# The loads of kept rows and of up's rows in the down stage: issued by SP instead of ScalarE

## The reference, cut to what matters

```
x = x + cross_attention(layernorm(x), ctx, mask)     # 16 batches of 64 tokens, 1601 keys
z = layernorm(x)                                     # 1024 tokens of 1024
s = silu(z @ w_gate.T)                               # 1024 x 2752
s = s with the 1376 smallest |s| of each row set to 0
x = x + (s * (z @ w_up.T)) @ w_down.T                # the down stage computes this product
x = x + mixture(layernorm(x))                        # top 2 of 8 low-rank experts
```

## Time and profile before

| | us |
|---|---|
| median of 3 runs (1389.53 to 1391.22) | 1389.76 |
| the profiled execution: its time | 1390.6 |
| the profiled execution: its span | 1388.8 |
| TensorE busy, of the span | 1338.2 (96%) |
| VectorE busy | 1019.0 (73%) |
| GpSimd busy | 894.5 (64%) |
| ScalarE busy | 804.5 (58%) |

### The profile page before, as it was taken

One profiled execution on the slowest core, in us unless ns is written; L12 is line 12 of the kernel. 1 busy time (PEld: TensorE's weight loads), 2 busy tenths in 40 slices (PEclk: granted clock), 3 DMA queues, 4 the chain that ended last, 5 costly groups with the idle time before them and its releaser, 6 DMA issues.

```text
span 1388.8 us, 30205 instructions
## 1 busy us (share of the span) xinstructions
PE 1338.2 (96%) x12535; PEld 990.2 (71%) x12535; DVE 1019.0 (73%) x1332; ACT 804.5 (58%) x1018; POOL 894.5 (64%) x561
## 2 busy tenths in 40 slices
PE   4999999999999999999999999999999999999897
PEld 3555555555555555589999998788888777887764
DVE  6888888888888888880000699996899885456555
ACT  6788888888888888843223742514234333343532
POOL 0799888888888888824433443242232798888571
PEclk9899999999999999999999999999999999999999
DMA  9022423232323232014336435797688799866452
GB/s 357 18 98 98 142 99 114 99 113 98 116 99 114 98 109 80 2 73 146 126 133 263 171 114 206 173 262 197 177 213 240 247 285 272 280 232 204 151 184 96
DMA packets 195586, 218.66 MB, mean 157 GB/s; under 512 B 96288, under 2 KB 169136, under 8 KB 191472
## 3 DMA queue, kind: packets, MB, share of 16 engines
q1 hardware_dynamic: 176736, 193.68, 43.4%
q10 hardware_dynamic: 18704, 22.96, 5.2%
HBM read 174.67 MB, written 41.94 MB: 156 GB/s over the span
## 4 chain that ended last, share of the span: by engine, by line
PE 77%; DVE 15%; ACT 3%; issue 2%; DMA 1%; POOL 1%; ACTq 0%; SPq 0%; POOLq 0%; DVEq 0%
PE fast_psum L2031 17%; PE fast_psum L2049 15%; PE fast_psum L2169 15%; PE fast_psum L2118 13%; PE fast_psum L2140 6%; PE fast_psum L2068 6%; DVE fast_below L1442 4%; PE fast_psum L2075 1%; DVE fast_near L1518 1%; DVE fast_top L1485 1%; PE fast_psum L2198 1%; PE fast_psum L2054 1%; PE fast_psum L2217 1%; DVE fast_near L1479 1%; DVE fast_near L1512 1%
## 5 line engine op out<-in xcount | busy, mean ns | idle before, releaser
L1372 DVE TENSOR_TENSOR fast_masked<-fast_psum,fast_mask_t 128x1024 f32<-128x1024 f32 (+1 forms) x416 | 488.4, 1219 | 72.4 <-PE fast_psum L2031 70.5
L1227 POOL TENSOR_TENSOR fast_pair<-fast_probs 128x1024 f32<-128x1024 f32 x192 | 456.9, 2383 | 96.9 <-PE fast_psum L2068 47.9
L1775 ACT ACTIVATE fast_probs<-fast_masked 128x1024 f32<-128x1024 f32 (+1 forms) x416 | 437.9, 1058 | 68.9 <-DVE fast_masked L1372 53.7
L1283 POOL TENSOR_TENSOR fast_d_lo<-fast_d_raw,fast_d_hi 128x256 fp32r<-128x256 f32 x252 | 217.7, 895 | 60.3 <-ACT fast_d_hi L1914 60.2
L2031 PE MATMUL fast_psum<-fast_qT,fast_kraw 32*128 32x256 f32 (+1 forms) x3328 | 247.1, 403 | 6.7 <-ACT fast_qT L1722 3.2
L2049 PE MATMUL fast_psum<-fast_probs,fast_vraw 128*32 128x256 f32 (+1 forms) x3328 | 226.6, 386 | 0.8 <-ACT fast_probs L1775 0.8
L2031 PEld LDWEIGHTS fast_psum<-fast_qT,fast_kraw 32*128 32x128 f32 (+1 forms) x3328 | 153.7, 182 | 93.2 <-DVE fast_masked L1372 53.9
L1260 POOL TENSOR_TENSOR fast_g_lo<-fast_g_raw,fast_g_hi 128x1408 fp32r<-128x1408 f32 x28 | 89.9, 3232 | 140.5 <-ACT fast_g_hi L1836 118.4
L2118 PE MATMUL fast_psum<-fast_g_hi,fast_z_hi 128*128 128x352 f32 x512 | 166.2, 325 | 0.0
L2118 PE MATMUL fast_psum<-fast_g_hi,fast_z_lo 128*128 128x352 f32 x512 | 165.9, 324 | 0.0
L1914 ACT CAST fast_d_hi<-fast_d_raw 128x1024 fp32r<-128x1024 f32 x66 | 69.3, 1051 | 165.8 <-PE fast_psum L2169 154.5
(11 more groups left out here) (174 smaller groups left out, 1930.5 us busy)
## 6 DMA issues: line engine op xcount, KB each, us to landing
fast_d_raw<-w_down SPq DMA_DIRECT2D x63, 512.0 KB, 4.3
fast_kraw<-ctx_t SPq DMA_DIRECT2D x32, 800.5 KB, 5.9
fast_vraw<-ctx_nat SPq DMA_DIRECT2D x16, 1536.0 KB
fast_g_raw<-w_gate_up SPq DMA_DIRECT2D x15, 1408.0 KB, 7.2
fast_mag<-s SPq DMA_DIRECT2D x9, 1376.0 KB, 8.3
fast_u_raw<-w_up_t SPq DMA_DIRECT2D x21, 512.0 KB, 6.5
u_t<-fast_u_out SPq DMA_DIRECT2D x42, 256.0 KB, 4.5
s<-fast_res SPq DMA_DIRECT2D x14, 704.0 KB, 3.8
```

Of the source, the lines that this page charges most:

```text
L1227: pool.tensor_tensor(pair[:, n % PAIR_BUFS], both[:, :, 0, :], both[:, :, 1, :], ALU.add).then_inc(paired, 1)
L1283: last = pool.tensor_tensor(low[rs, qs], d_raw[j][rs, qs], d_hi[j][rs, qs].bitcast(F32), ALU.subtract)
L1372: dve.tensor_tensor(into, of, m, ALU.add).then_inc(mask_added, 1)
L1775: act.activation(probs[0:r, g % RING, hp * HALF:(hp + 1) * HALF], masked[0:r, h % SLOTS, :], ACT.Exp).then_inc(exp_done, 1)
```

## The change

`load_factors` is moved out of ScalarE's program and takes the engine as its first argument. The first four loads are still issued by ScalarE. All others are issued by SP, at the same step n of its loop (for n+4), directly behind the weight load for n+3 and ahead of pieces, `load_x` and the loads of the last stage. The waits within are the same. Nothing else is changed.

```diff
--- before.py
+++ after.py
@@ -1012,6 +1012,27 @@
 
             return (0, 1) if t == 7 else (4, 5)
 
+        def load_factors(eng, n):
+            gi, k = divmod(n, IC)
+            if n >= TURNS:
+                eng.wait_ge(h_ready, n - TURNS + 1)
+            if k == 0:
+                stored = max(GROUPS[gi][-1] + 1, TILES - 2)
+                for j in range(2):
+                    eng.wait_ge(st_stored[j], 16 * QUARTERS * ((stored + 1 - j) // 2))
+            m, t0 = len(GROUPS[gi]), GROUPS[gi][0]
+            eng.dma_start(t_s[n % TURNS][0:rows(k), 0:m * P], s_t[k * P:k * P + rows(k), t0 * P:(t0 + m) * P]
+                          ).then_inc(ts_full[n % TURNS], 16)
+            if twice(n):
+                eng.dma_start(t_s[n % TURNS][UREST:P, 0:m * P], s_t[UF * P:I, t0 * P:(t0 + m) * P]
+                              ).then_inc(ts_full[n % TURNS], 16)
+                return
+            if gi == 0:
+                for i in (2 * k, 2 * k + 1):
+                    eng.wait_ge(u_stored[i % OUTS], 16 * (i // OUTS + 1))
+            eng.dma_start(t_u[n % TURNS][:, 0:m * P], u_t[k * P:(k + 1) * P, t0 * P:(t0 + m) * P]
+                          ).then_inc(tu_full[n % TURNS], 16)
+
         def load_k(sp, b):
             for u in range(2):
                 sp.dma_start(kraw[b % BUFS][:, u, :], ctx_t[2 * b + u]).then_inc(k_full[b % BUFS], 16)
@@ -1185,6 +1206,8 @@
             for n in range(STEPS):
                 if n + DS < STEPS:
                     load_down(n + DS)
+                if n + TURNS < STEPS:
+                    load_factors(sp, n + TURNS)
                 if n in DOWN_PIECE_AT:
                     store_piece(*DOWN_PIECE_AT[n])
                 if n in LOAD_X_AT:
@@ -1877,27 +1900,6 @@
                     for r in rounds:
                         compare(p, r)
 
-            def load_factors(n):
-                gi, k = divmod(n, IC)
-                if n >= TURNS:
-                    act.wait_ge(h_ready, n - TURNS + 1)
-                if k == 0:
-                    stored = max(GROUPS[gi][-1] + 1, TILES - 2)
-                    for j in range(2):
-                        act.wait_ge(st_stored[j], 16 * QUARTERS * ((stored + 1 - j) // 2))
-                m, t0 = len(GROUPS[gi]), GROUPS[gi][0]
-                act.dma_start(t_s[n % TURNS][0:rows(k), 0:m * P], s_t[k * P:k * P + rows(k), t0 * P:(t0 + m) * P]
-                              ).then_inc(ts_full[n % TURNS], 16)
-                if twice(n):
-                    act.dma_start(t_s[n % TURNS][UREST:P, 0:m * P], s_t[UF * P:I, t0 * P:(t0 + m) * P]
-                                  ).then_inc(ts_full[n % TURNS], 16)
-                    return
-                if gi == 0:
-                    for i in (2 * k, 2 * k + 1):
-                        act.wait_ge(u_stored[i % OUTS], 16 * (i // OUTS + 1))
-                act.dma_start(t_u[n % TURNS][:, 0:m * P], u_t[k * P:(k + 1) * P, t0 * P:(t0 + m) * P]
-                              ).then_inc(tu_full[n % TURNS], 16)
-
             def take_high(n):
                 gi, k = divmod(n, IC)
                 w = len(GROUPS[gi]) * P
@@ -1926,7 +1928,7 @@
                         compare(p, r)
                 if i == 2 * UF - 5:
                     for n in range(TURNS):
-                        load_factors(n)
+                        load_factors(act, n)
                 if i == 2 * UF - 3:
                     round_down(0)
                 if i == 2 * UF - 2:
@@ -1957,8 +1959,6 @@
             for n in range(STEPS):
                 if n >= 2:
                     take_high(n)
-                if n + TURNS < STEPS:
-                    load_factors(n + TURNS)
                 if n in ZT_AT:
                     take_zt(ZT_AT[n])
                 if n in PICK_AT:
```

## The result

The changed kernel takes 1395.22 us (median of 8 runs, 1391.57 to 1399.24), the kernel before beside it 1391.37 (8 runs, 1389.53 to 1393.79). The ratio is 1.0029 with a 95% interval of 1.0015 to 1.0043: about 4 us slower. Forecast were a median of 1390.3, half a us above the 1389.76 of the kernel before, and a range of 1387.0 to 1394.0. Of the 4.9 us between that median and 1395.22, 1.6 are the kernel before itself, which took 1391.37 here; 3.3 are what the forecast missed.

A forecast was written before the change was run, and what follows sets the result against it. TensorE was taken to bound the down stage, with 11.2 us of gaps. Terms 0 + 0 + 0 + 0.3 + 0.2 = +0.5 us took the profiled 1390.6 to 1391.1, median 1390.3, range 1387.0 to 1394.0.

The forecast's parts named there:

- What bounds the kernel: Down stage: TensorE is nearly always busy, so the change can pay only in its gaps, 11.2 us in all.
- ScalarE's side, 0: Some 49 us of issuing leave ScalarE, nearly all beside its other work, so nothing is gained: 0.
- the 5.95 us of the earlier trace: Sum of fourteen factor issues by ScalarE in the chain of waits, the most the change could gain there.
- rival B: Faster: ScalarE's issues are on the path, up to 5.95 us go, 1383.8, or 3.2 us, 1386.6; chance 0.14.
- The start, 0: Stage start: step 2's weights arrive when ScalarE's issues end, so removing the issues gives nothing: 0.
- Factors late, 0: SP issues factor loads later, but those of steps 6 and 14 still land before VectorE multiplies: 0.
- The steps with pieces, +0.3: Weights share SP's queue with factors; one pair delays them 1.4 us, under the cover: +0.3 us, bounds 0 and +3.6.
- a cover of 2.0: Time in hand in steps with pieces: 0.9 us from weight landing to `d_hi`, 1.1 more before TensorE starts.
- The 3.05 us of the earlier trace: Length of a weight issue on SP in the steps with pieces before the change, a queue without room.
- Step 25, +0.2: SP issues four last-stage loads there; the weights of step 29 may land later, 0 to +0.8 us for TensorE, taken +0.2.
- Rival A: Slower: weights stand behind factors, 1.4 us for each of four pieces less 2.0 covered; together +4.4, 1394.2; chance 0.20.
- Both of its signs: Weight landings above 8 us near 1125, and DMA-ended waits of `d_hi` above the present ones.

The follow-up runs named there:

- e4: The changed kernel with the pieces of tiles 6 and 7 issued by ScalarE, factors staying on SP: 0.9990 of the kernel before, timed again 0.9996.
- e13: The changed kernel with SP issuing the piece ahead of the two factor loads: 1.0052 of the kernel before.
- e5: The changed kernel with factor loads from step 4 on fetching only half the columns, as many issues, another product: 0.9992 of the kernel before.
- a0: The changed kernel timed again, nothing altered: 1.0022 of the kernel before.
- e1: The changed kernel with the factor pairs of loop steps 6 to 9 issued by ScalarE again: 1.0002 of the kernel before.
- e2: The changed kernel with the factor pairs of loop steps 6 to 9 and 25 issued by ScalarE again: 1.0006 of the kernel before.
- e10: The kernel before with the eight pieces issued by ScalarE behind its factor loads, SP issuing only weights: 1.0003 of the kernel before.
- e3: The changed kernel, all factor loads on SP, with the pieces at every second step: 1.0021 of the kernel before.
- e8: The changed kernel with two more SP loads of 128 rows x 8 bytes at steps 6 to 9 and 25: 1.0023 of the kernel before.
- e12: The kernel before, with each piece also waiting for VectorE's h_lo of the same step: 1.0000 of the kernel before.
- e15: The kernel before with 64 already fulfilled waits on SP between weights and piece: 1.0025 of the kernel before.
- e7: The kernel before with two more SP loads of 128 rows x 8 bytes at steps 6 to 9 and 25: 1.0013 of the kernel before.
- e9: The kernel before with two more SP loads of one row of 8 bytes at steps 6 to 9 and 25: 0.9999 of the kernel before.

## Why the prediction was wrong, by its steps

**What bounds the kernel** held: TensorE, with the gaps of the first and third window; the loss appeared as new gaps. **ScalarE's side, 0**, held: `zt` still 5.1 us, `d_hi` again 2.61 us idle for TensorE in ordinary steps. The chain of waits lost its fourteen factor issues by ScalarE and nothing was gained; in e4, where ScalarE issues no factors either and the pieces cost nothing, the two timings are 1.4 and 0.6 us below the kernel before, not 3.2 to 5.95. So the 5.95 us of the earlier trace rows were on no real path, and rival B is refuted. **The start, 0**: `d_hi` of step 2 is at 1090.11 after the change; the two profiles of the kernel before have it at 1088.88 and 1091.02, so no gain or loss can be told there. **Factors late, 0**: VectorE waited for no factor in the changed kernel; in e13 it did, 1.7 us.

**The steps with pieces, +0.3**, is the step that failed, and with it the whole forecast. It put the delay at 1.4 us for one pair, under a cover of 2.0, since the total backlog is the same and only the order differs. But the delay does not stay at one pair's: the four steps follow each other, and in each SP falls further behind GpSimd's release, by 0.2, 1.6, 3.5 and 4.5 us, where it had been on time. The cover of 2.0 us fits what was measured (e5, 2.4 us late, loses nothing that can be told); what was set against it was the delay of one pair in place of four. "SP is idle for most of a step" was read from ordinary steps: in those with pieces it was idle for 1.9, 1.4 and 0.6 us, and two issues with their gaps take 0.99, not 0.79. The 3.05 us of the earlier trace rows was the sign; I read it as a price already paid and not as SP's time in hand running out.

**Step 25, +0.2**: the load of step 29 idled 5.34 us after for 3.38 before. In this profile 1.5 of the second stretch's 1.9 us come between steps 28 and 32, and the chain has both factor issues of step 25 on it (0.32 and 0.99 us). But a0, with the same issues, is unchanged there, and the medians of e1 and e2, which differ in this pair alone, differ by 0.0004, within their intervals. No lasting cost is shown.

**Rival A** had the place and nearly the sum (+4.4 against +4.0, and +3.1 for a0), given a chance of 0.20. It added the delay of four pairs, which the forecast did not. Its working was half right: it priced the pair by its transfer, 1.4 us a piece; the periods grew by 1.0 (5.1 for 4.1), with 0.99 us of issuing in each. Both of its signs came. `d_hi` waits that a DMA ends went from 5 to 16. And the weight loads, counted from the start of their issue, land later: in tile 6 after 3.8, 4.4, 5.7, 6.1 and 7.0 us before, and after 3.7, 5.4, 7.4, 7.1 and 8.2 in the changed kernel. The last of them, for step 13:

```profile
L1126 SPq DMA_DIRECT2D fast_d_raw<-w_down x1: 3973/3973/3973, 1129.3 to 1129.3; - x1
...
DMA to landing us min/median/max: 8.2/8.2/8.2
```

So the weights were late for two reasons, the start of the issue (3.5 us for this load) and the landing (1.2 us more than before).

On the division of issues among engines, the Trainium skill ("DMA: Bandwidth & Descriptors", Issuing engines are not separate DMA queues) says that DMAs from all engines run on the same 16 DMA engines, and that starting them from several engines saves only the sequencer's time, which is usually small beside the DMA. In this kernel it was not small in the steps with pieces, where an issue is held for up to 4 us: all on SP came with 1.0029, and moving either the pieces or four pairs to ScalarE gave 0.9990 and 1.0002. Whether all of this is the sequencer's time no run tells; the measured difference decides.

## What to carry to other kernels

Before putting an issue on a queue, read that engine's own timeline where the change lands. A DMA issue much longer than its ordinary 0.33 us means that engine and queue hold each other up. Then take the engine's idle time in just these steps (here 1.9, 1.4, 0.6 us), not that of a stage, and compare it with what the new issues take (0.99 us), added up over all steps in a row; what doesn't fit must be less than what the loads have in hand (2.0 us here). The DMA share of a stage is a sum over queues and tells nothing of this. Keep a store of many short runs (here 2752 of 128 bytes) on a queue behind which nothing urgent is issued; e4 and e10 did so and lost nothing.

## What the runs showed of the hardware that was not expected

- The issue behind a piece ends 3.7 to 5.5 us after the start of the piece's issue in most kernels, up to 6.2 with pieces two steps apart (e3) and 3.2 to 3.7 with half the factor bytes (e5). Where SP had been away for 1 to 2 us before, it was at times only 2.4 to 3.0 (e8, e12, e15), but up to 4.6 in the same kernels. The piece itself is mostly issued in 0.33 to 0.43 us.
- With all on one queue the rate falls to 66 GB/s for a slice of 0.5 us between pieces. With the pieces on the other queue (e4) no slice after the sixth is under 200, and the mean of the 20 us is 299 GB/s for 238.
- Packet times of one queue can sum to more than the engines' time (104.3% for q1 from 1113.5 to 1132), so they overlap.
- 32 waits that were fulfilled cost SP 1.02 us less the 0.04 of the ordinary gap: 31 ns each.
- Two loads of 128 rows x 8 bytes (e7) cost 1.8 us of median over five steps, with an interval from 0 to 3.6, and two of one row (e9) nothing that can be told; the 0.33 us of G between them and the 127 rows were not tried apart.
